# Four products of ones in every step of an attention stage

## The chip, the cores and the metric

The kernel runs on one core of one Trainium2 chip. The metric is the device time of one launch, in microseconds (us). The engines are named as in the profile: PE is TensorE (matmuls), PEld its weight loads, DVE is VectorE, ACT is ScalarE, POOL is GpSimd and SP is SyncE, which here only issues DMAs. An "fp32r" product is a matmul on data rounded to a shorter fp32 form and runs in one pass. A plain fp32 matmul is recorded as two passes.

## The reference, cut to what matters

The reference has four parts that follow each other. For 64 samples it embeds an image-like input with three convolutions (128 rows of 64 numbers) and a text of 77 tokens with four small transformer layers (77 rows of 64 numbers), joins them to 205 rows, adds an attention over these rows, and adds a routed feed-forward layer. The attention, which is the part that the change touches, is for each sample

```
z = layernorm(h)                        # 205 x 64
q, k, v = z Wq' + bq, z Wk' + bk, z Wv' + bv     # 4 heads of 16
a = softmax(q k' / 4)                   # 205 x 205 for each head
h = h + bf16(a v) Wo' + bo
```

## The kernel before, in words

The kernel is written engine by engine, with semaphores between them. It has four stages: `image_branch`, `text_branch`, `fusion_attention` and `experts`. The joined rows `h` stay in SBUF for all 64 samples from the second stage on.

`fusion_attention` works on one sample at a time. The 205 rows are two tiles, of 128 and of 77 rows (`TILES`), called tile 0 and tile 1. The four heads lie in groups of 64 rows, two groups in each of two tensors (`A_GROUP` 64, `A_TENSORS` 2). Precision comes from splitting values into a high and a low part; low parts are stacked beside high ones, and masks on ACT (`low_k`, `low_q`) and a subtraction on DVE (`cut_k`, `cut_q`) make them.

The stage is a software pipeline written out by hand. Each engine has its own function `step(n)`, called for n from -4 to 65, and the order of the calls in it is the order of the work on that engine. No planner is involved. On PE a step is, in this order: `project_k(n+2)` (L1939, L1940), `project_o(n-2)` (L2038), `score(n+1, 1)` (L1976, tile 1), `weigh(n)` (L2011), `project_q(n+2)` (L1939, L1940 into bank `of_q`), `turn_max(n+1)` (L1985), `turn_outs(n)` (L2020), `turn_o(n-1)` (L2028), `score_t(n+1, 0)` (L1998, tile 0), `project_v(n+1)` (L1958, L1959), `turn_x(n+3)` (L1933), `score(n+2, 0)` (L1976, tile 0), `score_t(n+1, 1)` (L1998, tile 1).

The scores are made twice. `score` makes them with queries as rows, and DVE takes the negated maximum of each row from them (`find_max`, L1756, once for each tile). `turn_max` transposes the maxima on PE, `join_max` (L1765, DVE) adds them to the query operand and so makes `QP`, and `score_t` makes the scores again with keys as rows and the maximum already subtracted. ACT takes the exponential of these (`exp`, L1891, once for each tile) into `PT`, and `weigh` multiplies by the values.

The other work of ACT in a step is `low_k` (L1874), `copy_out` (L1896), `low_q` (L1882), `hi_x` (L1859), `set_oT` (L1903) and, at the end, `set_xT` (L1866, L1867), which copies the transposed rows of the sample that is projected next. The other work of DVE is `add_y` (L1803), the statistics (L1740, L1749), `cut_k` (L1773), `cut_q` (L1778), `normalise_o` (L1793, L1795) and `set_v` (L1785). POOL makes the normalised rows.

PSUM banks around the change: `scores_t` is two banks, the first (`scores_t[:, 0]`) written by `score_t` and read by `exp`. `of_q` is one bank, written by `project_q` and read by `low_q` and `cut_q`. A product with `start=True` overwrites what the bank held. Both of the bank's users above start their groups so.

`constants` runs once at the start of the kernel. It fills a few tiles on POOL and makes the identity matrix (`ident`) that all transposes use.

Of the kernel before, what the change touches and what calls it, by code (L numbers as in the profile page):

```python
# [9 lines left out]
BF16 = mybir.dt.bfloat16  # L10
# [5 lines left out]
P = 128  # L16
# [7 lines left out]
class Count:  # L24


    def __init__(self, base):
        self.base, self.k = base, 0
# [6 lines left out]
class Program:  # L35
# [22 lines left out]
    def end_stage(self):  # L58
        self.nc.clear_and_free_semaphores(self.stage)
        self.nc.all_engine_barrier()  # L60
        self.stage = None


def row(ap):
# [431 lines left out]
                each_quad(pe, step)  # L496


def constants(p, ident, clear):

    nc = p.nc
    cleared, made = p.sem("ident_cleared"), p.sem("ident_made")
    with nc.Block() as block:
        @block.gpsimd
        def _(pool):
            for t in clear:
                pool.memset(t[:], 0.0)
            pool.memset(ident[:], 0.0).then_inc(cleared, 1)
            pool.wait_ge(cleared, 1)
            pool.affine_select(out=ident[:], in_=ident[:], compare_op=ALU.not_equal, fill=1.0, base=0,  # L510
                               pattern=[[-1, P]], channel_multiplier=1).then_inc(made, 1)
            pool.wait_ge(made, 1)
# [996 lines left out]
def live(n):  # L1509

    return not isinstance(n, int) or 0 <= n < B
# [64 lines left out]
    last.then_inc(normed, 1)  # L1576


def fusion_attention(p, inputs, ident, rows_of, both_tiles):

# [7 lines left out]
    with ExitStack() as ctx:  # L1590
# [3 lines left out]
        def sem(name):  # L1594
            return p.sem("at_" + name)
# [27 lines left out]
        scores_t = p.psum(ctx, "at_scores_t", [P, 2, 512])  # L1623
# [4 lines left out]
        of_q = p.psum(ctx, "at_of_q", [P, 512])  # L1628
# [5 lines left out]
        with ExitStack() as setup:  # L1634
# [88 lines left out]
        k_made, k_low_set, k_cut, q_made, q_low_set, q_cut = (  # L1723
            sem("k_made"), sem("k_low_set"), sem("k_cut"), sem("q_made"), sem("q_low_set"), sem("q_cut"))
        v_made, v_set = sem("v_made"), sem("v_set")
        scored, max_set, max_turned, q_set = sem("scored"), sem("max_set"), sem("max_turned"), sem("q_set")
# [5 lines left out]
        with nc.Block() as block:  # L1732
# [186 lines left out]
            def _(pe):  # L1919
                held = {}  # L1920

                def take(bank, read, count):

                    if bank in held:
                        pe.wait_ge(*held[bank])
                    held[bank] = (read, count)
# [16 lines left out]
                def project_k(m):  # L1943
                    if live(m):
                        take("x_and_k", k_cut, m + 1)
                        project(m, k_rows, wk, k_made)

                def project_q(m):
                    if live(m):
                        pe.wait_ge(xT1_set, m + 1)  # L1950
                        take("of_q", q_cut, m + 1)
                        project(m, q_rows, wq, q_made)
# [10 lines left out]
                def score(m, tile):  # L1963
                    if live(m):
                        at, n = TILES[tile]
                        if tile == 0:
                            pe.wait_ge(k_cut, m + 1)
                            pe.wait_ge(q_cut, m + 1)
                            if m >= 1:
                                pe.wait_ge(q_set, m)  # L1970
                        else:
                            pe.wait_ge(max_set, m * 2 + 1)
                        for t in range(A_TENSORS):
                            for j in range(A_HPT):
                                head = slice(j * A_GROUP, (j + 1) * A_GROUP)
                                last = pe.matmul(scores[0:n, j, t * SEQP:(t + 1) * SEQP], QF[head, m % 2, t, at:at + n],  # L1976
                                                 KF[head, m % 2, t], start=True, stop=True)
                        last.then_inc(scored, 1)

                def turn_max(m):  # L1980
                    if live(m):
                        pe.wait_ge(max_set, m * 2 + 2)
                        for tile, (at, n) in enumerate(TILES):
                            for t in range(A_TENSORS):
                                last = pe.transpose(maxT[:, t, at:at + n], mpad[0:n, tile, t].bitcast(F32), ident[0:n, 0:n])  # L1985
                        last.then_inc(max_turned, 1)

                def score_t(m, tile):
                    if live(m):
                        at, n = TILES[tile]  # L1990
                        if tile == 0:
                            pe.wait_ge(q_set, m + 1)
                        if m * 2 + tile:
                            pe.wait_ge(exped, m * 2 + tile)
                        for t in range(A_TENSORS):
                            for j in range(A_HPT):
                                head = slice(j * A_GROUP, (j + 1) * A_GROUP)
                                last = pe.matmul(scores_t[0:n, j, t * SEQP:(t + 1) * SEQP], KF[head, m % 2, t, at:at + n],  # L1998
                                                 QP[head, m % 2, t], start=True, stop=True)
                        last.then_inc(scored_t, 1)  # L2000

                def weigh(m):
                    if live(m):
                        pe.wait_ge(exped, m * 2 + 2)
                        pe.wait_ge(v_set, m + 1)
                        if m >= 1:
                            pe.wait_ge(o_set, m)
                        for keys, (_, kn) in enumerate(TILES):
                            for h in range(A_HEADS):
                                t, j = h // A_HPT, h % A_HPT  # L2010
                                last = pe.matmul(outT[32 * h:32 * h + A_DH + 1, 0:SEQP], V[0:kn, m % 2, keys, h],  # L2011
                                                 PT[0:kn, keys, j, t * SEQP:(t + 1) * SEQP],
                                                 start=keys == 0, stop=keys == 1)
                        last.then_inc(weighed, 1)
# [17 lines left out]
                def project_o(m):  # L2032
                    if live(m):
                        pe.wait_ge(oT_set, m + 1)
                        take("v_and_y", y_added, m + 1)
                        for tile, (at, n) in enumerate(TILES):
                            for part in range(2):
                                last = pe.matmul(v_and_y[0:n, tile], oT[:, at:at + n], wo[:, part],  # L2038
                                                 start=part == 0, stop=part == 1)
                        last.then_inc(y_made, 1)  # L2040

                def step(n):
                    project_k(n + 2)
                    project_o(n - 2)
                    score(n + 1, 1)
                    weigh(n)
                    project_q(n + 2)
                    turn_max(n + 1)
                    turn_outs(n)
                    turn_o(n - 1)  # L2050
                    score_t(n + 1, 0)
                    project_v(n + 1)
                    turn_x(n + 3)
                    score(n + 2, 0)
                    score_t(n + 1, 1)
# [375 lines left out]
def early_fusion_embed(nc, x, x_txt, pos, weights, out):  # L2431

    def of(prefix, names):
        return {name: weights[prefix + name] for name in names}

    with ExitStack() as ctx:
        p = Program(nc, ctx, B)
        ident = p.sb("ident", [P, P])
        h = p.sb("h", [P, B, 2, D])
        h_img, h_txt = h[:, :, 0], h[0:S_TXT, :, 1]  # L2440

        def rows_of(n, tile, count=None):

            v = (h_txt if tile else h_img)[:, bass.ds(n, count or 1)]
            return v if count else v.rearrange("p a d -> p (a d)")

        text = TextInputs(p, x_txt, pos, of("L0_txt_", TEXT_WEIGHTS))
        attention = AttentionInputs(p, of("L0_attn_", ATTENTION_WEIGHTS))
        expert = ExpertInputs(p, of("L0_ffn_", EXPERT_WEIGHTS))
        constants(p, ident, [text.cols_all, attention.b_raw, expert.b_raw])  # L2450
        p.begin_stage()
        image_branch(p, x, of("L0_tok_", IMAGE_WEIGHTS), ident, h_img, h[D:P, :, 1], [text, attention, expert])
        p.end_stage()
        p.begin_stage()
        text_branch(p, text, ident, h_txt)
        p.end_stage()
        fusion_attention(p, attention, ident, rows_of, lambda n: h[:, n])
        experts(p, expert, ident, rows_of, out)


# [24 lines left out]
```

## Time and profile before

| what | value |
|---|---|
| median of 3 runs | 2515.48 us |
| lowest and highest run | 2495.77 and 2520.84 us |
| the profiled execution | 2517.77 us, its span 2516.0 us |
| granted TensorE clock, mean over the span | 0.835 |
| PE, PEld, DVE, ACT, POOL busy | 91%, 75%, 69%, 57%, 45% |

How to read it: the span is the time from the first to the last instruction of one execution, and the time of that execution is 1.8 us more. A granted clock of 1.00 is 2.4 GHz, one of 0.50 is 1.2 GHz, and values between are a stretch that had both. The image stage takes about the first 500 us, the text stage lasts to about 1505 us, the attention to about 2110 us and the experts to the end. The busy time of PE is modelled from pipelined matmuls, and counts the whole time that a product is under way.

### The profile page before, as it was taken

The page shows a single profiled execution, that of the slowest core. Times are in us where ns is not written, and L with a number is a line of the kernel's source. Part 1 is how long each engine was busy: PE and PEld are TensorE (multiplying, and loading weights), DVE is VectorE, ACT ScalarE, POOL GpSimd, SP SyncE. Part 2 cuts the span into 40 slices and gives each one's busy share as a digit, 9 for nine tenths or more (in the row PEclk, how much of TensorE's full clock was granted, in tenths as well). Part 3 has the DMA queues.
Part 4 walks back from the last instruction along what each step waited for, and adds up shares of the span by engine and source line. Part 5 has one row for each costly group of instructions (what it writes and reads, how often), then busy time and mean ns, then how long its engine had stood idle before and what let it go on. Part 6 is the DMA issues. An engine that isn't in the chain of part 4 may idle for free. (4 is left out here: it accounts for less than half of the span.)

```text
span 2516.0 us, 58817 instructions
## 1 busy us (share of the span) xinstructions
PE 2279.1 (91%) x20145; PEld 1889.1 (75%) x20145; DVE 1736.5 (69%) x5336; ACT 1437.5 (57%) x3034; POOL 1144.1 (45%) x1519
## 2 busy tenths in 40 slices
PE   6999999848999999999999709999999996999998
PEld 6999999747888888888888606777777774666665
DVE  5655555356888888888888655555555554788888
ACT  2222222106888888888888644444444444666663
POOL 4433333105777777777777562222222222434432
PEclk8999999857999999999999855555555555999999
DMA  2000031000000000000000000000000000000000
GB/s 85 15 18 13 13 67 25 1 0 2 2 2 2 2 2 2 2 2 2 2 2 2 2 0 1 1 1 1 1 1 1 1 1 1 8 10 9 8 10 11
DMA packets 38894, 21.13 MB, mean 8 GB/s; under 512 B 28696, under 2 KB 38040, under 8 KB 38554
## 3 DMA queue, kind: packets, MB, share of 16 engines
q1 hardware_dynamic: 38654, 17.97, 2.9%
q8 instruction: 145, 2.38, 0.4%
q14 instruction: 95, 0.78, 0.1%
HBM read 14.60 MB, written 3.36 MB: 7 GB/s over the span
## 5 line engine op out<-in xcount | busy, mean ns | idle before, releaser
L441 PE MATMUL im_c<-im_a_hi,im_w 128*128 128x256 f32 (+2 forms) x1920 | 428.8, 318 | 13.8 <-POOL im_a_lo L351 13.8
L441 PEld LDWEIGHTS im_c<-im_a_hi,im_w 128*128 128x128 f32 x1920 | 322.1, 191 | 30.9 <-POOL im_a_lo L351 14.0
L441 PE MATMUL im_c<-im_a_lo,im_w 128*128 128x256 f32 (+2 forms) x960 | 303.8, 316 | 0.0
L1043 POOL TENSOR_TENSOR tx_KB<-tx_KF,tx_head_rows 128x1248 fp32r<-128x1248 f32 x128 | 289.6, 2263 | 23.3 <-PE tx_scores_t L1328 15.2
L1842 POOL TENSOR_TENSOR at_xs<-at_z,at_xs 128x128 fp32r<-128x128 f32 x64 | 29.0, 453 | 421.9 <-ACT at_xs L1859 421.9
L904 DVE TENSOR_REDUCE tx_mpad<-tx_scores 77x8 fp32r<-77x616 f32 x256 | 202.1, 789 | 2.9 <-PE tx_maxT L1316 1.9
L345 POOL TENSOR_TENSOR im_rstd<-im_var_eps,im_power 128x4 f32<-128x4 f32 x64 | 68.6, 1072 | 284.1 <-DVE im_var_eps L280 284.1
L441 PEld LDWEIGHTS im_c<-im_a_lo,im_w 128*128 128x128 f32 x960 | 183.1, 191 | 8.4
L1174 ACT ACTIVATE tx_PT<-tx_scores_t 77x624 f32<-77x624 f32 x256 | 175.8, 687 | 17.1 <-PE tx_scores_t L1328 4.6
L1328 PE MATMUL tx_scores_t<-tx_QP,tx_KB 128*77 128x78 f32 x2048 | 183.9, 240 | 0.0
L274 DVE BATCH_NORM_STATS2 im_stats<-im_h 128x6 f32<-128x128 f32 (+1 forms) x192 | 47.6, 303 | 192.0 <-ACT im_h L386 111.9
L1328 PEld LDWEIGHTS tx_scores_t<-tx_QP,tx_KB 128*77 128x77 f32 x2048 | 172.4, 150 | 9.2 <-issue 0.3
L2359 PE MATMUL ex_y<-ex_wd,ex_H_hi 128*128 128x512 f32 (+1 forms) x512 | 171.9, 417 | 0.0
L1756 DVE TENSOR_REDUCE at_mpad<-at_scores 128x4 fp32r<-128x820 f32 (+1 forms) x128 | 129.5, 1012 | 56.1 <-PE at_scores L1976 55.0
L1891 ACT ACTIVATE at_PT<-at_scores_t 128x824 f32<-128x824 f32 (+1 forms) x128 | 109.5, 855 | 62.9 <-PE at_scores_t L1998 62.9
L380 ACT ACTIVATE im_a_hi<-im_normed 128x192 fp32r<-128x192 f32 (+1 forms) x192 | 63.0, 348 | 137.8 <-DVE im_normed L298 135.5
L2248 DVE TENSOR_REDUCE ex_summed<-ex_weighted 128x64 f32<-128x512 f32 (+1 forms) x128 | 135.6, 1059 | 4.4
L1035 POOL TENSOR_TENSOR tx_xs_f<-h,tx_xs_f 77x256 fp32r<-77x256 f32 x64 | 46.6, 728 | 200.6 <-ACT tx_xs_f L1124 200.6
L1306 PE MATMUL tx_scores<-tx_KB,tx_QF 128*77 128x312 f32 x512 | 126.1, 328 | 1.3 <-DVE tx_mpad L904 1.2
L1566 POOL TENSOR_TENSOR ex_rstd<-ex_var_eps,ex_power 128x2 f32<-128x2 f32 x64 | 44.5, 696 | 181.7 <-DVE ex_var_eps L1531 181.7
L1342 PE MATMUL tx_out_bank<-tx_PT,tx_V 128*9 128x78 f32 x4096 | 118.1, 233 | 8.8 <-DVE tx_o_rows L926 2.3
L351 POOL TENSOR_TENSOR im_a_lo<-im_normed,im_a_hi 128x192 fp32r<-128x192 f32 (+1 forms) x192 | 93.6, 517 | 52.4 <-ACT im_a_hi L380 52.4
(316 smaller groups left out, 6472.0 us busy)
## 6 DMA issues: line engine op xcount, KB each, us to landing
im_x<-x SPq DMA_DIRECT2D x16, 384.0 KB, 3.3
out<-h SPq DMA_DIRECT2D x32, 64.0 KB
tx_toks<-x_txt SPq DMA_DIRECT2D x1, 1925.0 KB
im_raw<-L_tok_conv_w SPq DMA_DIRECT2D x1, 1280.0 KB, 8.6
out<-h SPq DMA_DIRECT2D x32, 38.5 KB
im_raw<-L_tok_conv_w SPq DMA_DIRECT2D x1, 960.0 KB, 4.6
im_raw<-L_tok_conv_w SPq DMA_DIRECT2D x1, 640.0 KB, 5.9
tx_raw_W<-L_txt_W SPq DMA_DIRECT2D x2, 256.0 KB, 6.8
```

Source lines behind the costliest of these rows:

```text
L351: last = pool.tensor_tensor(a_lo[c][:, par, b, :, 2:2 + J], normed[:, b, 0:cols * J].rearrange("p (d j) -> p d j", d=cols), a_hi[c][:, par ...
L441: last = pe.matmul(acc[:, :, d0:d1], w[c][:, slot, part], img[:, b0_:b1_, d0 + shift:d1 + shift, kj:kj + J], start=opens, stop=closes)
L904: dve.tensor_reduce(mpad[0:R].rearrange("p t (j r) -> p t j r", r=GROUP)[:, :, :, 3 * DH], scores[0:R, :, 0:HPT * SP_TXT].rearrange("p t ( ...
L1043: pool.tensor_tensor(KB[:, q % 2, t], KF[:, t].bitcast(F32).unsqueeze(1).broadcast_to([P, HPT, QW]), head_rows[:].unsqueeze(2).broadcast_t ...
L1174: act.activation(PT[0:R, b % 2], scores_t[0:R, :, 0:HPT * SP_TXT], ACT.Exp, scale=SCALE)\
L1306: last = pe.matmul(scores[0:R, t, 0:HPT * SP_TXT], QF[:, q % 2, t, b, 0:R], k, start=True, stop=True)
L1328: last = pe.matmul(scores_t[0:R, t, j * SP_TXT:(j + 1) * SP_TXT], k, QP[:, b % 2, t], start=True, stop=True)
L1342: last = pe.matmul(outT[32 * j:32 * j + DH + 1, t], V[:, q % 2, b, t * HPT + j], PT[:, b % 2, t, j * SP_TXT:(j + 1) * SP_TXT], start=True, ...
L1756: dve.tensor_reduce(mpad[0:n, tile].rearrange("p t (j r) -> p j t r", r=A_GROUP)[:, :, :, 3 * A_DH], scores[0:n, :, 0:WIDE].rearrange("p j ...
L1891: act.activation(PT[0:n, tile], scores_t[0:n, :, 0:WIDE], ACT.Exp, scale=SCALE).then_inc(exped, 1)
L2248: dve.tensor_reduce(summed[0:n, tile], weighted[0:n, tile].rearrange("p e d -> p d e"), AX.X, ALU.add)\
L2359: last = pe.matmul(acc, h[:, slot, half, at:at + n], wd[:, part, half, 0:WIDE], start=False, stop=half == HALVES - 1 and h is H_lo)
```

## The change

The change adds a tile of ones in bf16, 128 by 512 (`Warm.rows`), which POOL fills once at the start. In each step of the attention, PE issues four products of 128x128 ones with 128x512 ones. Two of them go into `scores_t[:, 0]` right before `score_t` of tile 0, and two into `of_q` between `project_o` and `score` of tile 1. All four start a new sum, so the real products that follow in the same bank overwrite them, and nobody reads them. The pair in `of_q` waits until `cut_q` of the sample before has read the bank, the pair in `scores_t` until the exponential before has. In `score_t` of tile 0 the wait for `QP` is moved behind the pair. The order of all other work is as it was.

```diff
+class Warm:
+    def __init__(self, p):
+        self.rows = p.sb("warm_rows", [P, 512], BF16)
+
+    def run(self, pe, bank, times):
+        for _ in range(times):
+            pe.matmul(bank, self.rows[:, 0:P], self.rows[:], start=True, stop=True)
...
             for t in clear:
                 pool.memset(t[:], 0.0)
+            pool.memset(warm.rows[:], 1.0)
             pool.memset(ident[:], 0.0).then_inc(cleared, 1)
...
                 def score_t(m, tile):
                     if live(m):
                         at, n = TILES[tile]
-                        if tile == 0:
-                            pe.wait_ge(q_set, m + 1)
                         if m * 2 + tile:
                             pe.wait_ge(exped, m * 2 + tile)
+                        if tile == 0:
+                            warm.run(pe, scores_t[:, 0], 2)
+                            pe.wait_ge(q_set, m + 1)
                         for t in range(A_TENSORS):
...
+                def keep_warm(m):
+                    if live(m):
+                        if m >= 1:
+                            pe.wait_ge(q_cut, m)
+                        warm.run(pe, of_q[:], 2)
+
                 def step(n):
                     project_k(n + 2)
                     project_o(n - 2)
+                    keep_warm(n + 2)
                     score(n + 1, 1)
                     weigh(n)
```

## Rows read from the trace of the kernel before

**Rows 1.** The page, the span in 40 slices: the granted clock in tenths
```profile
PEclk8999999857999999999999855555555555999999
```

**Rows 2.** Busy time in stretches: us, PE, PEld, DVE, ACT, POOL, granted clock, DMA share, GB/s
```profile
580.00:590.00 10.00, 10.00 (x82) 8.99 (x82) 3.74 (x11) 4.60 (x9) 0.66 (x1) 0.50 0.01 2
590.00:600.00 10.00, 9.43 (x130) 8.23 (x133) 7.71 (x21) 5.52 (x13) 6.60 (x5) 0.89 0.01 2
...
900.00:910.00 10.00, 9.81 (x139) 8.80 (x138) 9.31 (x30) 8.56 (x20) 6.63 (x7) 1.00 0.01 2
...
1430.00:1440.00 10.00, 4.99 (x31) 3.96 (x29) 3.72 (x14) 3.35 (x8) 4.09 (x5) 0.59 0.01 2
...
1560.00:2080.00 520.00, 515.62 (x3266) 389.75 (x3264) 279.27 (x730) 255.92 (x508) 121.13 (x281) 0.50 0.00 1
...
2102.00:2104.00 2.00, 1.19 (x16) 0.89 (x20) 0.48 (x2) 1.14 (x2) 0.00 (x0) 1.00 0.00 0
```

**Rows 3.** Timeline of one attention step: start us, us, instruction, idle before
```profile
1899.96 0.75 PE L1998 MATMUL at_scores_t<-at_QP,at_KF 64*128 64x206 f32 x4
...
1901.98 0.34 ACT L1866 ACTIVATE at_xT<-at_x_and_k 128x205 fp32r<-128x205 f32 x1 [0.37 <-PE at_x_and_k L1933]
1902.22 0.32 ACT L1867 ACTIVATE at_xT<-at_x_and_k 64x205 fp32r<-64x205 f32 x1
...
1902.67 1.01 DVE L1756 TENSOR_REDUCE at_mpad<-at_scores 128x4 fp32r<-128x820 f32 x1 [0.81 <-PE at_scores L1976]
...
1904.58 0.63 PE L1976 MATMUL at_scores<-at_KF,at_QF 64*77 64x206 f32 x4
...
1908.54 0.58 DVE L1765 TENSOR_TENSOR at_QP<-at_scores,at_QF 128x410 fp32r<-128x410 f32 x1 [1.79 <-PE at_scores L1985]
...
1909.18 0.76 PE L1998 MATMUL at_scores_t<-at_QP,at_KF 64*128 64x206 f32 x4
```

**Rows 4.** Groups of weight loads, attention, 1560 to 2080 us
```profile
L1998 PEld LDWEIGHTS at_scores_t<-at_QP,at_KF 64*77 64x77 f32 x452 | 52.2, 277 | 17.1 <-DVE at_QP L1765 17.1
```

**Rows 5.** Timeline of PE and ACT, last attention steps
```profile
2097.78 1.57 PE L2011 MATMUL at_outT<-at_PT,at_V 128*17 128x206 f32 x16
2099.29 0.95 PE L1985 MATMUL at_scores<-ident,at_mpad 128*128 128x128 f32 x4
...
2100.91 0.47 PE L1998 MATMUL at_scores_t<-at_QP,at_KF 64*128 64x206 f32 x4
...
2101.43 0.86 ACT L1891 ACTIVATE at_PT<-at_scores_t 128x824 f32<-128x824 f32 x1 [0.22 <-PE at_scores_t L1998]
...
2102.34 0.41 PE L1998 MATMUL at_scores_t<-at_QP,at_KF 64*77 64x206 f32 x4 [0.47 <-ACT at_PT L1891]
...
2102.68 0.55 PE L2038 MATMUL at_v_and_y<-at_wo,at_oT 65*128 65x64 f32 x4
2102.80 0.85 ACT L1891 ACTIVATE at_PT<-at_scores_t 77x824 f32<-77x824 f32 x1 [0.51 <-PE at_scores_t L1998]
```

**Rows 6.** Timeline of PE in the experts, at either clock
```profile
2147.14 1.05 PE L2359 MATMUL ex_y<-ex_wd,ex_H_hi 128*128 128x512 f32 x2
2148.00 0.63 PE L2359 MATMUL ex_y<-ex_wd,ex_H_lo 128*128 128x512 f32 x1
...
2149.93 0.39 PE L2359 MATMUL ex_y<-ex_wd,ex_H_lo 128*77 128x512 f32 x1
2150.16 0.63 PE L2359 MATMUL ex_y<-ex_wd,ex_H_hi 128*77 128x512 f32 x2
...
2200.36 0.34 PE L2389 MATMUL ex_turned_x<-ident,ex_xs 128*128 128x128 f32 x2
...
2203.25 0.61 PE L2371 MATMUL ex_up<-ex_xT,ex_w 128*128 128x206 f32 x4
2203.79 0.50 PE L2356 MATMUL ex_y<-ex_biases,ex_ones 33*128 33x512 f32 x1
```

**Rows 7.** Timeline of POOL at the start
```profile
0.82 0.58 POOL L507 MEMSET at_b_raw<- 97x576 f32 x1
```

More of the change, by code:

```diff
@@ L496, in _, with constants @@
                 each_quad(pe, step)
-def constants(p, ident, clear):
+def constants(p, ident, warm, clear):
     nc = p.nc
@@ L1576, in norm_rows, with fusion_attention @@
     last.then_inc(normed, 1)
-def fusion_attention(p, inputs, ident, rows_of, both_tiles):
+def fusion_attention(p, inputs, ident, warm, rows_of, both_tiles):
     nc = p.nc
@@ L2449, in early_fusion_embed @@
         expert = ExpertInputs(p, of("L0_ffn_", EXPERT_WEIGHTS))
-        constants(p, ident, [text.cols_all, attention.b_raw, expert.b_raw])
+        warm = Warm(p)
+        constants(p, ident, warm, [text.cols_all, attention.b_raw, expert.b_raw])
         p.begin_stage()
@@ L2456, in early_fusion_embed @@
         p.end_stage()
-        fusion_attention(p, attention, ident, rows_of, lambda n: h[:, n])
+        fusion_attention(p, attention, ident, warm, rows_of, lambda n: h[:, n])
         experts(p, expert, ident, rows_of, out)
```

## The prediction

> **What bounds the kernel now.** I read the page's slices first, for the granted clock. It is at nine tenths or more through the image and text stages and in the experts, and at five tenths over the whole attention [rows 1]. The stretches say it sharper: between 1560 and 2080 us the clock is 0.50 throughout, that is 1.2 of 2.4 GHz, and PE is busy 515.6 of 520 us, against 279.3 for DVE and 255.9 for ACT [rows 2]. So the attention is bound by PE, and by a PE at half speed.
>
> The timeline of one step gives the period: `score_t` of tile 0 starts at 1899.96 and again at 1909.18 us, 9.22 us later [rows 3]. 64 samples make 590 us. In 520 us there are 56.4 such steps, so DVE works 4.95 us and ACT 4.54 us per step. Neither could bind before the period has come down to about half.
>
> PE is not quite dense. The weight loads of `score_t` wait 17.1 us in 520 us for `QP` [rows 4], 0.30 us per step, the only wait of PE that the groups put down to another engine. Other gaps are hidden in the modelled ends.
>
> **What the clock followed.** The profile's busy share alone does not decide it. In the text stage PE was busy 10.00 of 10 us at 0.50, and the clock rose in the next 10 us; there it then stayed at 1.00 with PE busy 9.81 of 10 us [rows 2]. In the attention 99% busy never raised it. It did rise once, at the stage's very end: the rows before are `weigh` with the transposes of the maxima right behind it, since the last sample has no `project_q` between them [rows 5]; afterwards the stretch from 2102 us shows 1.00 [rows 2]. So what came ahead of that rise was denser than the middle of the stage by a missing `project_q`, whose products are set apart by their weight loads. It fell around the end of the text stage, when PE was busy 4.99 of 10 us [rows 2].
>
> **The change, part by part.**
>
> *The price of a product of ones.* No row shows a bf16 product of 512 columns. The nearest are the experts' fp32r products of 512 columns: two and then the next start at 2147.14 and 2148.00, 0.43 us each at half clock; 2149.93 and 2150.16, 0.23 us each at full clock [rows 6]. Four per step cost 1.71 us or 0.92 us of PE. A bf16 product might cost less at its edges; I bound it by nothing below and by the full-duration 0.63 us above, and take the spacing, because they are issued back to back.
>
> *The pair before `score_t`.* PE waits 0.30 us there for `QP` anyway [rows 4], so at half clock the pair adds 0.86 - 0.30 = 0.56 us. Moving the wait for `QP` behind the pair is what hides them; the wait for the exponential now ahead of it is long over (that exponential ended before `weigh`). Queued behind are `score_t`, `project_v` and the rest of the step, all late by the same amount.
>
> *The pair before `score` of tile 1.* Nothing hides it. The maximum of tile 0 that this score needs started at 1902.67 and took 1.01 us, so it was there at 1903.68, and the score started at 1904.58 only because PE was occupied [rows 3]. The pair costs its whole 0.86 us. Its wait for `cut_q` is for the sample before, done within the previous step, and costs nothing.
>
> *Half clock, therefore:* 9.22 + 0.56 + 0.86 = 10.64 us per step, 1.42 us more.
>
> *Full clock.* PE's own work is (9.22 - 0.30) / 2 + 0.92 = 5.4 us, above DVE and ACT. But then the loop through the other engines is longer. From the start of `score_t` of tile 0 to the exponential 0.52 (2100.91 to 2101.43), the exponential 0.86 [rows 5], `set_xT` 0.56 (1901.98 to 1902.54 [rows 3]), a handover 0.05, `project_k` 0.54 (2203.25 to 2203.79 for four products [rows 6]), `project_o` 0.45 (its four last 0.55 with their ends [rows 5]), the pair 0.46, the score of tile 1 to its maximum 0.46 (like 2102.34 to 2102.80 [rows 5]), the maximum 1.01 [rows 3], a handover 0.05, the four transposes to `QP` 0.60 (two last 0.34, the second 0.11 behind the first, so four 0.56, and a handover [rows 6]), `QP` 0.58 [rows 3], a handover 0.06. The sum is 6.20 us. The other pair stands beside the 0.60 and 0.58 of this loop and is hidden. I take 6.2 us per step. From below it is bounded by PE's 5.4 us; from above I allow 0.1 us more at each of 13 places, 7.5 us.
>
> *Does the clock rise?* The products of ones run back to back on the whole array. The pair before `score_t` stands behind three groups that already run nearly without a gap (`turn_max`, `turn_outs`, `turn_o`), fills the 0.30 us hole behind them and adds 0.56 us. That run is as long and as dense as `weigh` with the transposes, which came ahead of the rise at the stage's end [rows 5]. I take it that the clock rises, and after about 4 steps, some 40 us: the text stage went up after at least 10 us of solid work [rows 2], and here only a part of each step is solid.
>
> The Trainium skill (TensorE: Matmul & The Clock Gate, "What's actually happening") has it that sustained matmul activity releases the throttle. By this rule the attention, busy 99%, would long be at full clock and the products would have nothing to release; the trace disagrees, 0.50 over 520 us [rows 2]. By the rule alone the products are pure work, and the sum would be the first rival's, 2607 us.
>
> *Does it stay up?* The text stage kept 1.00 with real gaps. At full clock the stretch from `score_t` to `project_o` is the sparse one, since PE there waits for the exponential and for `set_xT`; the pair in `of_q` stands at its end. I expect it to hold.
>
> *The fill of the tile of ones* is on POOL ahead of `ident`, at the start where all wait. A fill of 97x576 fp32 took 0.58 us [rows 7]; this one has 128x512 bf16. I take 0.5 us, from nothing to 0.6.
>
> **The sum**, against the profiled execution's 2517.77 us (2.3 us above the median of the runs shown): 64 steps lose 9.22 - 6.20 = 3.02 us, 193 us. Four steps before the rise cost 4 x (10.64 - 6.20) = 18 us of that. With the fill, 2517.8 - 193 + 18 + 0.5 = 2343 us, or 2341 us against the median. With 5.4 us per step in the 60 fast steps it is 48 us less, 2293 us; with 7.5 us it is 78 us more, 2419 us.
>
> **Rivals.**
>
> *The clock stays at half (slower).* Place: every step; price 64 x 1.42 = 91 us; 2607 us against the median. For it: 56 steps with PE 99% busy never raised the clock [rows 2], and the pairs go in at two places, neither beside the other. Against it: the rise at 2100 us. It decides when fewer than about a third of the steps run at full clock, 1.42 / (1.42 + 3.02) = 0.32.
>
> *The clock goes up and down.* At full clock PE gets through its work sooner and then waits for DVE and ACT in every step, and those waits could bring it down again. With half of the steps at each, the mean step is 8.4 us and the time 2515.5 - 51 + 0.5 = 2465 us. The clock did fall again at the stage's end, where PE was busy 1.19 of 2 us [rows 2]. Against it: the text stage at 1.00. The Trainium skill (same page, "A second HAM failure mode: psum-queue depth-cycling") tells of such a to and fro where matmul groups alternate over PSUM banks with small idles between; no row of this stage shows it.
>
> *Another engine becomes the bound.* The loop through ACT and DVE is longer than my sum, for instance because `low_k`, `copy_out` and `low_q` push `set_xT` back. At 7.5 us per step this is the 2419 us above.
>
> *The products do nothing.* They are hidden or cheap and the clock is as before: 2515 us. Against it: PE has 0.30 us of wait per step and no more.
>
> **Chances.** My forecast 0.69, the slower loop 0.05, up and down 0.07, no effect 0.03, half clock 0.16. The predicted time is the forecast's, 2341 us. The range, 2288 to 2470 us, starts under the forecast's lower bound of 2293 us, holds its upper one, the slower loop, a late rise (each step more at half clock is 4.44 us) and the clock that goes up and down, and leaves out half clock and no effect, 0.19 together. The forecast's own range is 2293 to 2419 us. A difference of under 1% can't be told from none on this kernel. Faster by more than 1%: 0.69 + 0.05 + 0.07 = 0.81. Within: 0.03. Slower: 0.16.
>
> **What would show it.** The granted clock of the changed kernel is 1.00 in the attention from shortly after its start. The step, from one `score_t` of tile 0 to the next, is near 6.2 us. ACT's wait before `exp` shrinks little and PE shows waits for `at_xT` and for `at_mpad`. The products of ones start 0.21 to 0.23 us apart. The times of the image, text and experts stages are as before to a few us. The forecast is wrong if the clock reads 0.50 in the attention with a step near 10.6 us, or if it changes between both.

## The result and the profile after

The changed kernel takes 2329.53 us (median of 4 runs, 2329.0 to 2336.02). The kernel before, timed beside it and earlier, takes 2510.64 us (median of 4). The ratio is 0.9289, with a 95% interval of 0.9236 to 0.9342: 7% faster. The span of the profiled execution went from 2516.0 to 2327.2 us. Here and below a ratio is the time over that of the kernel before, timed beside it, and the interval behind it is the 95% one; the median of the kernel before differed between the groups of runs (2506 to 2520 us), so small differences between groups mean little.

The first view is the slices of the page of the changed kernel (its granted clock in tenths), to be held against [rows 1].

```profile
PEclk8999999975999999999999998589999996999999
```

The run of fives that was the attention is gone. What is left of half clock lies between the stages. The busy times in stretches say the same in the columns of [rows 2].

```profile
1511.00:1530.00 19.00, 16.64 (x82) 10.78 (x82) 7.71 (x18) 8.55 (x16) 6.11 (x15) 0.50 0.00 1
1530.00:1560.00 30.00, 29.83 (x300) 20.47 (x296) 23.61 (x65) 20.80 (x44) 10.69 (x25) 1.00 0.01 2
...
1560.00:1900.00 340.00, 338.34 (x3434) 233.26 (x3429) 273.44 (x715) 231.84 (x497) 117.54 (x275) 1.00 0.01 2
```

The clock is 0.50 for the first 19 us of the stage and 1.00 from then until about 5 us before its last product has ended. PE's busy share is 99% at 1.00 here, as it was at 0.50 in the kernel before [rows 2], so in this stage that share does not tell the two levels apart.

The timeline of one step of the changed kernel, beside [rows 3]; columns are start, duration, instruction, idle before and what ended it.

```profile
1700.50 0.61 PE L72 MATMUL at_of_q<-warm_rows 128*128 128x512 bf16 x2
...
1701.04 0.42 PE L1988 MATMUL at_scores<-at_KF,at_QF 64*77 64x206 f32 x4
...
1701.50 1.01 DVE L1768 TENSOR_REDUCE at_mpad<-at_scores 77x4 fp32r<-77x820 f32 x1 [0.25 <-PE at_scores L1988]
...
1702.75 0.52 PE L1997 MATMUL at_scores<-ident,at_mpad 128*128 128x128 f32 x4
...
1703.31 0.58 DVE L1777 TENSOR_TENSOR at_QP<-at_scores,at_QF 128x410 fp32r<-128x410 f32 x1 [0.30 <-PE at_scores L1997]
...
1703.42 0.59 PE L72 MATMUL at_scores_t<-warm_rows 128*128 128x512 bf16 x2
...
1703.95 0.47 PE L2011 MATMUL at_scores_t<-at_QP,at_KF 64*128 64x206 f32 x4
...
1704.46 0.86 ACT L1903 ACTIVATE at_PT<-at_scores_t 128x824 f32<-128x824 f32 x1 [0.39 <-PE at_scores_t L2011]
...
1705.21 0.34 ACT L1878 ACTIVATE at_xT<-at_x_and_k 128x205 fp32r<-128x205 f32 x1
...
1705.82 0.36 PE L1951 MATMUL at_x_and_k<-at_xT,at_wk 128*128 128x206 f32 x1
...
1706.35 0.46 PE L2051 MATMUL at_v_and_y<-at_wo,at_oT 65*128 65x64 f32 x4
...
1706.65 0.61 PE L72 MATMUL at_of_q<-warm_rows 128*128 128x512 bf16 x2
```

From one pair in `of_q` (1700.50) to the next (1706.65) the step is 6.15 us, where it was 9.22 us [rows 3]. The whole gain lies in this stage: its first product starts 1511.9 us into the old span and 1511.2 us into the new, and its last ends at 2109.1 and 1920.5 us. The stage went from 597.2 to 409.3 us, 187.9 of the span's 188.8 us.

### The profile page after: what moved, and what is told of

It reads as the page before. It is cut to its first block and busy times, and to the rows that moved or that the text cites. A ratio compares the mean times of both kernels' runs of the same rounds, so it can differ in the third digit from the quotient of the medians.

```text
span 2327.2 us, 59267 instructions
## 1 busy us (share of the span) xinstructions
PE 2091.1 (90%) x20401; PEld 1720.2 (74%) x20401; DVE 1735.5 (75%) x5336; ACT 1419.1 (61%) x3034; POOL 1144.9 (49%) x1520
```

## The experiments

In all of them the step is read as the distance of two `join_max` rows (L1777, `at_QP`) of DVE, one per sample. The diffs are against the changed kernel and are cut to the lines that count; a left-out part is marked with three dots.

**The order of the waits alone.**

```diff
                         if tile == 0:
-                            warm.run(pe, scores_t[:, 0], 2)
                             pe.wait_ge(q_set, m + 1)
...
-                    keep_warm(n + 2)
```

> Leaves out all four products; keeps the moved wait for QP and the tile of ones. Theory A (the clock gives the gain): nothing raises the clock, the attention reads 0.50, the step stays at 9.22 us, the time within 0.5% of 2511 us. Rival B (the gain comes from the order of the two waits in score_t): faster by tens of us with the clock at 0.50.

Measured: 2524.17 us (10 runs, nine from 2523 to 2526 and one at 2488), ratio 1.0058 (1.0015 to 1.0100). The clock reads 0.50 over the attention, and the step is 9.32 us. Timeline of DVE:

```profile
1706.29 0.58 DVE L1777 TENSOR_TENSOR at_QP<-at_scores,at_QF 128x410 fp32r<-128x410 f32 x1 [1.80 <-PE at_scores L1997]
1715.61 0.58 DVE L1777 TENSOR_TENSOR at_QP<-at_scores,at_QF 128x410 fp32r<-128x410 f32 x1 [1.79 <-PE at_scores L1997]
```

The moved wait gives nothing. It costs 0.09 us per step, 6 us in all, which I had put at nothing; the two profiled executions, 2523.49 and 2517.77 us, differ by as much. (The rest of the 0.6% lies in runs of the kernel before at 2494 to 2506 us.) Why it costs this is not settled. All experiments below carry it, so 9.32 us is their base at half clock.

**Each pair alone.** First the pair in `of_q`:

```diff
                         if tile == 0:
-                            warm.run(pe, scores_t[:, 0], 2)
                             pe.wait_ge(q_set, m + 1)
```

> Keeps the pair in of_q alone. Theory A1 (the clock rises on the long dense run that ends in the pair before score_t, so that pair is the one needed): the clock stays at 0.50, the pair costs its whole 0.86 us, step 10.08 us, 2511 + 55 = 2566 us. Rival A2 (any pair is enough, since what was missing is only more products per step): the clock rises, step about 6.1 us because this pair stands in the loop through ACT and DVE, about 2330 us.

Measured: six runs from 2519 to 2544 us, ratio 1.0100 (1.0045 to 1.0155), and two at 2567 and 2569 us; the median of all eight is 2544.01 us. Stretches of its trace, taken in a run of 2525 us:

```profile
1560.00:1580.00 20.00, 18.31 (x193) 13.52 (x194) 15.91 (x40) 13.82 (x31) 7.12 (x17) 1.00 0.01 2
1700.00:1900.00 200.00, 191.96 (x1161) 138.30 (x1178) 97.76 (x256) 88.70 (x176) 43.20 (x100) 0.50 0.00 1
```

and its steps, the first two at full clock and the last two at half:

```profile
1564.12 0.58 DVE L1777 TENSOR_TENSOR at_QP<-at_scores,at_QF 128x410 fp32r<-128x410 f32 x1 [0.30 <-PE at_scores L1997]
1570.36 0.58 DVE L1777 TENSOR_TENSOR at_QP<-at_scores,at_QF 128x410 fp32r<-128x410 f32 x1 [0.30 <-PE at_scores L1997]
...
1703.48 0.58 DVE L1777 TENSOR_TENSOR at_QP<-at_scores,at_QF 128x410 fp32r<-128x410 f32 x1 [1.79 <-PE at_scores L1997]
1713.68 0.58 DVE L1777 TENSOR_TENSOR at_QP<-at_scores,at_QF 128x410 fp32r<-128x410 f32 x1 [1.79 <-PE at_scores L1997]
```

The clock rose early, held for 8 steps (one of 5.93 and seven of 6.24 us), fell, was at half for 46 steps of 10.20 us, and came back only for the last seven. So this pair does not hold the clock, and at half clock it costs 10.20 - 9.32 = 0.88 us. The expectation said 10.08 us from a base of 9.22; its pair was 0.86 us. The two runs above, near the 2566 us of that expectation, have a mean clock of 0.832 and 0.833 where the other six have 0.843 to 0.855; no trace shows whether the clock rose in them at all.

Now the pair in `scores_t`:

```diff
                 def step(n):
                     project_k(n + 2)
                     project_o(n - 2)
-                    keep_warm(n + 2)
                     score(n + 1, 1)
```

> Keeps the pair in scores_t alone. Theory A1: the clock rises as with both; the pair in of_q was 0.46 us of the loop of 6.2 us, so the step falls to about 5.8 us and the time to 2330 - 60 x 0.35 = 2309 us, provided the clock holds. If the sparse stretch from score_t to project_o needs the other pair, the clock goes up and down and the time is between 2400 and 2500 us. Rival (both pairs are needed for the rise): clock 0.50, step 9.22 + 0.56 = 9.78 us, 2547 us.

Measured: 2303.98 us (2 runs), ratio 0.9195 (0.9116 to 0.9275). In 5 further runs of the same kernel:

> The same as the kernel with the pair in scores_t alone, timed in more rounds and beside the kernel below that adds products in the experts. Step 5.70 us, 2304 us, ratio to before 0.915 to 0.925. If the clock holds less surely without the pair in of_q, some runs lie tens of us above the others.

Measured: 2310.75 us (2305.59 to 2311.41), ratio 0.9197 (0.9171 to 0.9222). A step of the first of the two traces:

```profile
1704.05 0.58 DVE L1777 TENSOR_TENSOR at_QP<-at_scores,at_QF 128x410 fp32r<-128x410 f32 x1 [0.20 <-PE at_scores L1997]
1709.75 0.58 DVE L1777 TENSOR_TENSOR at_QP<-at_scores,at_QF 128x410 fp32r<-128x410 f32 x1 [0.20 <-PE at_scores L1997]
```

The step is 5.70 us, and the clock is 1.00 from 1539 us to the stage's last products. In the other trace it is 1.00 from 1549 us, and the attention ends 4.9 us later; that is most of the 7.0 us between the two profiled executions. Half of the change is enough, and the other half costs 0.45 us per step in the loop.

The later rise leaves one whole step with the pair at half clock, the clock reading 0.50 from 1537 to 1548 us:

```profile
1537.91 0.58 DVE L1777 TENSOR_TENSOR at_QP<-at_scores,at_QF 128x410 fp32r<-128x410 f32 x1 [1.80 <-PE at_scores L1997]
1547.84 0.58 DVE L1777 TENSOR_TENSOR at_QP<-at_scores,at_QF 128x410 fp32r<-128x410 f32 x1 [1.79 <-PE at_scores L1997]
```

It takes 9.93 us (9.95 and 9.94 us in the traces of the last two experiments below), so at half clock this pair costs 9.93 - 9.32 = 0.61 us.

**Products in the first eight samples only.**

```diff
-                            warm.run(pe, scores_t[:, 0], 2)
+                            warm.run(pe, scores_t[:, 0], 2 if m < 8 else 0)
...
-                        warm.run(pe, of_q[:], 2)
+                        warm.run(pe, of_q[:], 2 if m < 8 else 0)
```

> Both pairs in the first 8 samples only, none in the other 56. Theory H1 (the products are needed to raise the clock, not to hold it; the text stage held it with gaps): 1.00 to the end, the step without products about 5.8 us, 2330 - 56 x 0.35 = 2310 us. Rival H2 (they are needed to hold it): the clock falls soon after the eighth sample and stays at 0.50, step 9.22 us again, gain only 8 x 3 = 24 us or less, about 2490 us.

Measured: 2479.01 us (4 runs; three near 2479, one 2426). In the trace of one of the three, steps without products, at full and later at half clock:

```profile
1585.26 0.58 DVE L1777 TENSOR_TENSOR at_QP<-at_scores,at_QF 128x410 fp32r<-128x410 f32 x1 [0.21 <-PE at_scores L1997]
1591.05 0.58 DVE L1777 TENSOR_TENSOR at_QP<-at_scores,at_QF 128x410 fp32r<-128x410 f32 x1 [0.20 <-PE at_scores L1997]
...
1708.94 0.58 DVE L1777 TENSOR_TENSOR at_QP<-at_scores,at_QF 128x410 fp32r<-128x410 f32 x1 [1.79 <-PE at_scores L1997]
1718.26 0.58 DVE L1777 TENSOR_TENSOR at_QP<-at_scores,at_QF 128x410 fp32r<-128x410 f32 x1 [1.79 <-PE at_scores L1997]
```

Without products the step is 5.79 us at full clock. The clock held for two steps with the pair in `scores_t` alone and six with no product, fell at 1612 us and did not rise again in the attention; 47 steps ran at 9.32 us. The run at 2426 us left no trace. Its mean clock is 0.884 against 0.856 to 0.858, and its 53 us less are worth 15 of these steps at full clock (an estimate, 53 / (9.32 - 5.79)), so it too lost the clock for about half of the stage. The products are needed to hold it. Against the 5.70 us with the pair, they take no time at full clock; why the step without them is 0.09 us longer is as open as the 0.09 us of the moved wait.

**One product.**

```diff
-                            warm.run(pe, scores_t[:, 0], 2)
+                            warm.run(pe, scores_t[:, 0], 1)
...
-                    keep_warm(n + 2)
```

> One product of ones in scores_t instead of two, none in of_q. It still stands in the wait for QP. Theory D (the amount at this place decides, and one is too little, as none was): the clock rises now and then and falls back, as with none after the eighth sample; at least half of the steps at 9.3 to 9.5 us, time 2400 to 2550 us. Rival (any filling of the wait for QP is enough): step 5.70 us throughout, 2304 us.

Measured: 2538.36 us (3 runs), ratio 1.0070 (1.0047 to 1.0093).

```profile
1701.14 0.59 DVE L1777 TENSOR_TENSOR at_QP<-at_scores,at_QF 128x410 fp32r<-128x410 f32 x1 [1.79 <-PE at_scores L1997]
1710.65 0.58 DVE L1777 TENSOR_TENSOR at_QP<-at_scores,at_QF 128x410 fp32r<-128x410 f32 x1 [1.79 <-PE at_scores L1997]
```

From the third step on each takes 9.51 us, and the clock is at half from end to end. The expectation had it rising now and then; it never did. One product does not raise it and costs 0.19 us. Between one and two the kernel goes from 0.7% slower to 8% faster than the kernel before.

**Four in one place.** In `scores_t`:

```diff
-                            warm.run(pe, scores_t[:, 0], 2)
+                            warm.run(pe, scores_t[:, 0], 4)
...
-                    keep_warm(n + 2)
```

> Four products in scores_t, none in of_q: the same number as the change, all in one place. At full clock the wait for QP behind the first two is still 0.42 us in the trace, so two more of 0.22 us just fit: step 5.70 to 5.8 us and about 2306 us if they are free; step 6.15 us and 2330 us if a product costs PE its time wherever it stands.

Measured: 2327.11 us (2 runs), ratio 0.9234 (0.9207 to 0.9261), step 6.13 us (1701.03 to 1707.16 us), clock 1.00 from 1524 us. So the third and fourth product are not free. In `of_q`:

```diff
                         if tile == 0:
-                            warm.run(pe, scores_t[:, 0], 2)
                             pe.wait_ge(q_set, m + 1)
...
-                        warm.run(pe, of_q[:], 2)
+                        warm.run(pe, of_q[:], 4)
```

> Four products in of_q between project_o and the score of tile 1, none in scores_t: the number of the change, all in the place where two did not hold the clock. Theory D (the number per step decides): the clock holds, and since this place is in the loop through ACT and DVE the step is 6.24 + 0.43 = 6.67 us, 2304 + 60 x 0.97 = 2362 us. Theory P (the place decides, and here the products stand apart from the dense run of weigh to turn_o): the clock falls back, steps of 10.2 + 0.86 = 11.1 us for most of the stage, about 2600 us.

Measured: 2374.55 us (2 runs), ratio 0.9459 (0.9422 to 0.9496), step 6.67 us, and five short falls of the clock, ten samples apart, each of which makes one step 8.2 to 8.3 us. The first of these stretches is one of them:

```profile
1623.00:1626.00 3.00, 2.94 (x19) 1.12 (x22) 1.26 (x4) 0.27 (x1) 0.00 (x0) 0.50 0.00 0
1626.00:1691.00 65.00, 59.54 (x595) 42.71 (x598) 48.26 (x127) 41.47 (x90) 21.33 (x50) 1.00 0.01 2
```

The step is what the first theory of the expectation gave, and the falls, 5 x 1.6 = 8 us, are most of the 12 us by which the time is above its 2362 us. Both the number and the place count. Four in `of_q` hold the clock, but for short falls, where two there lost it; in `scores_t` two and four held it without a fall.

**The pair before `project_q`.**

```diff
                     project_o(n - 2)
-                    keep_warm(n + 2)
                     score(n + 1, 1)
                     weigh(n)
+                    keep_warm(n + 2)
                     project_q(n + 2)
```

and none in `scores_t`.

> The pair in of_q moved to right before project_q, behind weigh, where PE otherwise stops for 0.3 us; none in scores_t. The same two products per step as the pair that stood between project_o and the score of tile 1 and held the clock for 8 steps only. Theory P (place decides: the pair must join work that is dense already, and here it makes one dense run of weigh, products, project_q and turn_max): the clock rises and holds, step 5.8 to 6.1 us, about 2320 us. Rival (the pair must stand behind the transposes, or stop the wait for QP): clock mostly 0.50, step 9.33 + 0.86 = 10.2 us, about 2560 us.

Measured: 2340.39 us (2 runs), ratio 0.9287 (0.9260 to 0.9314). Stretches:

```profile
1541.00:1613.00 72.00, 64.44 (x690) 50.60 (x699) 56.50 (x151) 49.63 (x107) 25.61 (x60) 1.00 0.01 2
1613.00:1616.00 3.00, 2.67 (x23) 1.41 (x24) 2.05 (x5) 0.78 (x2) 0.00 (x0) 0.50 0.00 0
1617.00:1657.00 40.00, 35.66 (x382) 27.86 (x386) 31.97 (x86) 27.87 (x61) 14.94 (x35) 1.00 0.01 2
1657.00:1660.00 3.00, 2.67 (x27) 1.43 (x27) 2.22 (x6) 1.20 (x3) 0.00 (x0) 0.53 0.03 5
```

Here the clock goes up and down, as a rival of the prediction had it. But each of its five falls lasts only about 3 us and makes one step 7.63 us in place of 6.13. Behind `weigh` the pair came with a rise within 3 us after each fall; in front of `score` the clock stayed down for 46 steps.

**Products of a sixteenth of the array.** The pair in `scores_t` alone, with

```diff
-            pe.matmul(bank, self.rows[:, 0:P], self.rows[:], start=True, stop=True)
+            pe.matmul(bank[0:32], self.rows[0:32, 0:32], self.rows[0:32], start=True, stop=True)
```

> The pair in scores_t with 32x32 ones as weights and 32 rows of 512 moving, so that each product takes as long but uses a sixteenth of the array. If what counts is that PE streams columns, the clock rises and holds as with whole products: step 5.70 us, 2304 us. If it counts how much of the array works, it stays at half: step about 9.75 us, 2545 us.

Measured: 2451.67 and 2571.89 us. In the trace of the first:

```profile
1560.00:1840.00 280.00, 280.00 (x1677) 196.47 (x1676) 138.14 (x361) 126.41 (x251) 60.01 (x139) 0.50 0.00 1
1840.00:2000.00 160.00, 159.19 (x1649) 114.84 (x1648) 134.04 (x359) 116.04 (x250) 59.78 (x140) 1.00 0.01 2
```

Neither theory holds as it stood. The clock stays at half for 30 steps of 10.04 us, rises without anything in the program having changed, and is back at half for the last steps. A small product takes about as long as a whole one (616 ns against 634 ns, medians of the few in the first steps, at half clock), and the pair adds 0.72 us to the step at half clock where the whole pair added 0.61. So the time that the products take is not all that counts: in these two runs small products did less for the clock than whole ones did in seven. Small products may be worth more than none, or that rise was chance; with two runs this stays open. What the operands hold was not tried: every added product was of ones.

**An early start.** The pair in `scores_t` in every step, and

```diff
                     last.then_inc(turned, 1)
+                    warm.run(pe, of_q[:], 16)
...
+                warm.run(pe, of_q[:], 10)
                 for n in range(-4, B + 2):
                     step(n)
```

> The pair in scores_t in every step, and 16 products in the stage's setup and 10 more ahead of the first step, where PE idles 11 us. The clock should read 1.00 when the first sample is projected. The pair alone had two steps at 8.8 and 9.2 us; at 5.7 us each this is 6 to 7 us less: 2297 us. Rival (the fill is bound by the other engines, or the clock falls again in the sparse first steps): 2304 us, or longer by what the 16 products hold up the setup.

Measured: 2312.74 us (2 runs), ratio 0.9177 (0.9151 to 0.9204). Stretches at the stage's start:

```profile
1501.00:1507.00 6.00, 5.89 (x15) 2.07 (x14) 5.68 (x32) 0.20 (x1) 3.65 (x11) 0.54 0.01 1
1507.00:1513.00 6.00, 2.90 (x13) 1.11 (x12) 2.88 (x15) 0.64 (x3) 2.91 (x7) 1.00 0.00 0
1514.00:1551.00 37.00, 34.60 (x197) 24.62 (x199) 19.16 (x49) 18.30 (x35) 9.36 (x24) 0.50 0.00 1
```

The clock rose at the end of the 16 products, which ran back to back for 6.1 us, and it was at 0.50 again from 1514 us, after a stretch in which PE was busy for half of the time, the ten further products among it. The first steps then ran at half clock as before. The Trainium skill (TensorE: Matmul & The Clock Gate, "What's actually happening") states that activity releases the throttle and idle time brings it back. The trace agrees with the first half; before the fall PE was not idle but busy for 2.90 of 6 us. The early rise was lost before the dense steps began, and the kernel gained nothing (2310.75 us without it).

**The same in the experts.** The pair in `scores_t`, and in PE's part of `experts`, which is now handed the tile of ones,

```diff
                         m, slot = n + 5, (k + 5) % 8
+                        if isinstance(n, int) and n < 0:
+                            warm.run(pe, y[0].rearrange("p e d -> p (e d)"), 4)
                         pe.wait_ge(h_cut, m + 1)
```

> The pair in scores_t in the attention, and in the experts four products of ones in each step before the first sample is finished (n < 0), into the bank y[0] that nobody uses yet, ahead of the wait for h_cut where PE idles 1.9 us at half clock. The experts have 44 us at half clock at their start. If the clock rises some 25 us earlier, PE's 2.7 us of work in each of these steps halves: 4 x 1.3 us and 4 us of the first dense step, 2304 - 8 = 2296 us. Rival (these steps are bound by POOL and ACT, the products only add): 2304 to 2310 us.

Measured: 2304.43 us (5 runs, 2299.91 to 2305.51), ratio 0.9173 (0.9147 to 0.9198), against 2310.75 us (2305.59 to 2311.41) for the pair in `scores_t` alone in the same rounds. The same stretch, first without and then with these products:

```profile
1921.00:1945.00 24.00, 18.35 (x75) 13.20 (x74) 8.08 (x31) 14.81 (x36) 8.78 (x15) 0.50 0.00 1
```

```profile
1921.00:1945.00 24.00, 20.65 (x118) 13.66 (x118) 12.81 (x44) 18.77 (x47) 11.51 (x20) 0.99 0.00 1
```

The clock rises 24 us sooner, and the time from the attention's last product to the end falls from 409.3 to 402.7 us. By the medians it is 6 us ahead of the pair alone, with the ranges of the two just apart, and 25 us under the change. But 6 us is 0.3%, about either kernel's own spread, and two earlier runs of the pair alone gave 2303.98 us.

## Why the prediction was right, point by point

- **The clock is what pays: right.** It was 1.00 through the stage, and the wait moved without products gave nothing. Wherever the clock stayed at half, products made the step longer.
- **The step at full clock: right.** 6.20 forecast, 6.15 measured. The loop's terms read off the new timeline: from `score_t` (1703.95) to the exponential it takes 0.51, to `set_xT` 0.75, to `project_k` 0.61, to `project_o` 0.53, to the pair 0.30, to the score 0.54, to its maximum 0.46. There the forecast's path is not quite the one that ran. The maximum is done at 1702.51, but the transposes start at 1702.75, because PE is still at `weigh` and `project_q`. From score to transposes it takes 1.71 us, not 1.52. The pair and `project_o` together took 0.84, not 0.91 us, and the overlap of `exp` with `set_xT` gave back another 0.1 us. Errors of both signs cancelled, so that the sum came within 0.05 us is in part luck.
- **How soon it rises: too late.** I charged four steps at half clock, 18 us. The changed kernel has one step of 8.54 us and then 5.85 and 6.15. This is the largest error of the sum, which was some 12 us over the median of 2329.53. Without that charge it would have been 2325 - 2 = 2323 us, 6 us under the median.
- **The price at half clock: slightly too low.** 0.88 us for the pair in `of_q` where I had 0.86, 0.61 us for that in `scores_t` where I had 0.56, and 0.09 us for the moved wait where I had nothing. Two pairs at half clock would have made some 10.8 us rather than 10.64 (a sum of separate runs; no kernel held both at half clock for long). The slower rival would have been at about 2618 us, not 2607: an estimate, 64 steps of 1.6 us more.
- **Why it stays up: wrong reason.** I had put this on the pair in `of_q`, at the end of the sparse stretch. That pair alone lost the clock after 8 steps, and the one in `scores_t` alone kept it. For the rise I had named the pair in `scores_t`; it does both. That the clock would hold was right, but partly by luck: the pair that does it was in the change beside the one that I had credited.
- **The hidden pair: right.** With none the full-clock step is 5.79 us, with the pair 5.70. What I had not seen is that the room is used up by it: two more cost 6.13 - 5.70 = 0.43 us. In the expectation for four products in `scores_t` I had read the 0.42 us that the weight loads of `score_t` wait for `QP` as free time of PE. PE was streaming ones in that time; idle time of PEld is not idle time of PE.
- **The up-and-down rival** is real in this stage, with the pair before `project_q` and with four products in `of_q`, though with falls of 3 us rather than half of the steps.
- **The signs that I had named: not all came.** PE waits for `at_xT` (12.9 us in 55 steps) and the second product of a pair starts 0.21 us behind the first (a pair takes 0.59 us, one product 0.38). But no wait for `at_mpad` shows, since PE is busy when the maximum is done, and ACT's wait before `exp` did not shrink little: it went from 0.97 to 0.39 us per step.
- **The fill of ones: right.** It took 0.52 us, and the fill of `ident` behind it starts 0.46 us later, at 2.26 instead of 1.80 us, where I had 0.5:

```profile
1.80 0.52 POOL L519 MEMSET warm_rows<- 128x512 bf16 x1
2.26 0.20 POOL L520 MEMSET ident<- 128x128 f32 x1
```

## What to carry to other kernels

Look at the granted clock of each stage before anything else: this stage was bound by PE at 0.50, and its step went from 9.22 to 5.70 us, a factor of 1.6, once the clock was up. The busy share did not show that. Here products of ones paid best in a wait that PE had anyway, next to its densest run, with two of them; try the number and the place one by one, since one too few cost time and gained nothing. Then take out those that the clock does not need: here half of them were 0.45 us per step of pure loss.

## What was not expected of the hardware

The clock has two answers to the same program. Once it was up, six steps without products ran at 5.79 us, and then it was at half for 47 of the same steps. With small products it sat at half for 30 steps and then held for 27. The steps at either level are alike to about 0.01 us, so it is not the load that drifts. The kernel before shows a trace of this: 19 runs beside the first experiments lie between 2494 and 2521 us, with a mean clock from 0.834 to 0.846 that goes with the time. Why a run takes the one or the other was not tried.
